# A new slot order, a tail written out by hand, and part of the x1 and weight splitting on GpSimd, in a fused attention and mixture-of-experts kernel

## The reference

```python
# x [8, 256, 128] f32, w_qkv [384, 128], w_out [128, 128], 16 heads of 8, window 128
q, k, v = split(x @ w_qkv.T)                       # to heads
att = where(sliding_window_mask, q @ k.T / sqrt(8), -inf)
x1 = layernorm(x + (softmax(att) @ v) @ w_out.T)
# mixture of 8 experts over the 2048 tokens, the best 2 by softmax(x1 @ router_w)
y = sum over e in top2: p_e * (gelu(x1 @ w_in[e] + b_in[e]) @ w_out[e] + b_out[e])
out = layernorm(x1 + y)
```

## Time and profile before

| | |
|---|---|
| median of the runs | 197.1 us |
| profiled execution, its own time | 196.5 us |
| its span, first to last instruction | 194.8 us |
| busy: PE, weight loads, DVE | 169.4, 121.5, 154.8 us |
| busy: ACT, POOL | 114.6, 84.1 us |
| mean granted TensorE clock | 0.994 of full speed |
| DMA | 17.25 MB, 35% of 16 engines' span |

### The profile page before, as it was taken

How to read it: one execution, slowest core, us unless ns; L and a number is a source line. 1 busy time by engine, 2 the same in 40 slices (tenths; PEclk the granted TensorE clock), 3 DMA queues, 4 the chain that set the end, 5 groups by cost and what they waited for, 6 DMA issues and landing times. The chain is left out here.

```text
span 194.8 us, 6184 instructions
## 1 busy us (share of the span) xinstructions
PE 169.4 (87%) x2450; PEld 121.5 (62%) x2460; DVE 154.8 (79%) x468; ACT 114.6 (59%) x216; POOL 84.1 (43%) x157
## 2 busy tenths in 40 slices
PE   7579887988989989889999899989999979999950
PEld 3354454655656656556656544558988869999950
DVE  6985959669598698697988999635798869898793
ACT  4542056687686766876857757564353784564720
POOL 7960006556563655746738366561043002603003
PEclk9999999999999999999999999999999999999997
DMA  5589594194780882955901000000000000020011
GB/s 142 148 232 222 168 242 132 53 212 125 158 226 11 176 206 72 214 160 110 218 13 57 2 8 0 3 0 0 5 0 0 3 27 27 0 59 0 3 53 54
DMA packets 23127, 17.25 MB, mean 89 GB/s; under 512 B 1827, under 2 KB 21179, under 8 KB 23099
## 3 DMA queue, kind: packets, MB, share of 16 engines
q1 hardware_dynamic: 23099, 16.87, 35.2%
HBM read 9.35 MB, written 7.34 MB: 86 GB/s over the span
## 5 line engine op out<-in xcount | busy, mean ns | idle before, releaser
L486 ACT ACTIVATE probs<-st 128x768 f32<-128x768 f32 x59 | 47.9, 811 | 23.8 <-PE st L1067 20.6
L443 POOL TENSOR_SCALAR_AFFINE_SELECT probs<-probs 128x1024 f32<-128x1024 f32 x32 | 35.1, 1097 | 57.4 <-ACT probs L486 57.3
L713 DVE TENSOR_REDUCE max_parts<-score_banks 128x2 f32<-128x384 f32 x64 | 32.6, 550 | 4.6 <-PE score_banks L1041 4.2
L594 ACT ACTIVATE hid<-score_banks,b_in_sb 128x512 f32<-128x512 f32 x32 | 21.9, 687 | 21.0 <-PE score_banks L1173 20.9
L716 DVE TENSOR_REDUCE max_parts<-score_banks 128x4 f32<-128x512 f32 x32 | 20.6, 686 | 13.6 <-PE score_banks L1041 13.6
L1067 PE MATMUL st<-stack 51*64 51x256 bf16 (+1 forms) x472 | 21.2, 254 | 6.2 <-ACT probs L486 5.7
L1030 PE MATMUL score_banks<-edges,ident_bf 64*64 64x256 bf16 (+1 forms) x192 | 19.0, 296 | 4.5 <-DVE max_parts L713 3.4
L1089 PE MATMUL o_bank<-probs,v 128*32 128x256 f32 x256 | 20.4, 391 | 0.0
L445 POOL TENSOR_SCALAR_AFFINE_SELECT probs<-probs 128x512 f32<-128x512 f32 x32 | 20.3, 634 | 0.0
L1067 PEld LDWEIGHTS st<-stack 51*64 51x64 bf16 (+1 forms) x472 | 8.6, 104 | 18.7 <-ACT probs L486 11.8
L860 DVE SCALAR_TENSOR_TENSOR x_rows<-st,gate,x_rows 128x128 f32<-128x128 f32 x64 | 18.1, 344 | 2.4 <-PE st L1187 2.0
(11 more groups left out here) (136 smaller groups left out, 331.2 us busy)
## 6 DMA issues: line engine op xcount, KB each, us to landing
stack<-scratch SPq DMA_DIRECT2D x28, 192.0 KB, 4.0
scratch<-parts SPq DMA_DIRECT2D x16, 192.0 KB, 4.0
scratch<-parts SPq DMA_DIRECT2D x24, 128.0 KB, 3.8
x_rows<-x SPq DMA_DIRECT2D x4, 256.0 KB, 5.6
out<-y_sb SPq DMA_DIRECT2D x8, 128.0 KB, 1.8
x_t_sb<-x_t SPq DMA_DIRECT2D x3, 256.0 KB, 4.8
w_in_sb<-w_in SPq DMA_DIRECT2D x1, 512.0 KB, 5.8
w_out_sb<-w_out SPq DMA_DIRECT2D x1, 512.0 KB, 7.9
```

The lines of the kernel that those rows point to most:

```text
L443: pool.affine_select(out=own, in_=own, compare_op=ALU.is_ge, fill=0.0, base=0, pattern=[[0, 2], [0, 4], [1, P]], channel_multiplier=-1).th ...
L486: nc.scalar.activation(probs[g][:, :, two, :].rearrange("p k j c -> p j k c"), pair_banks(PAIRS * b + p)[:, :, 0:3 * P].rearrange("p j (k ...
L594: nc.scalar.activation(hid[e % 2][:, :], hid_bank[e % 2], ACT.Gelu_apprx_tanh, bias=b_in_sb[:, e:e + 1]).then_inc(gelu_done, 1)
L713: nc.vector.tensor_reduce(top[:, 1, r, pair:pair + 2], bank[:, 0:384].rearrange("p (h c) -> p h c", h=2), X_AXIS, ALU.max, negate=True).th ...
```

## The change

The slot constants move, and the loops of PE, ACT, DVE and POOL end at slot 63. What came in slots 64 to 74 is written out in an order of its own on each engine, and `keep_warm` in it is gone. In the loop, PE does a slot's `scores` ahead of its `turned_scores`, and DVE a slot's maxima ahead of everything else. The turned output moves to misc[0], the turned attention, x1 and logits to misc[1] (of the last batch, x1 to misc[0]), with the waits that go with it. POOL takes `split_x1` of batches 0 to 4 (`share_x1`, in slot 6, two slots behind `turn_x1` in slot 4), and the weight splitting in eight pieces, one expert each, in slots 46 to 60; the load of `w_in` gets a semaphore of its own. DVE keeps `split_x1` of batches 5, 6 and 7.

```diff
-TURN_MAX, VALUES, S2, PV = 8, 12, 11, 15
-COPY_O, TURN_O, TURN_ATTN, PROJECT_OUT, TURN_X1, LOGITS = 22, 23, 25, 26, 30, 31
-PROJECT_QK, STACK = -14, -8
+TURN_MAX, VALUES, S2, PV = 8, 10, 11, 15
+COPY_O, TURN_O, TURN_ATTN, PROJECT_OUT, TURN_X1, LOGITS, SHARE_X1 = 21, 22, 23, 24, 28, 30, 30
+PROJECT_QK, SUBTRACT, STACK = -14, -12, -8
+WEIGHT_SLOTS = (46, 48, 50, 52, 54, 56, 58, 60)
...
# POOL
+            def share_x1(b):
+
+                cols = slice(b * T, (b + 1) * T)
+                pool.wait_ge(x1_copied, b + 1)
+                pool.tensor_copy(x1_hi[:, cols], x1_t[:, :]).then_inc(x1_hi_done, 1)
+                pool.wait_ge(x1_hi_done, b + 1)
+                pool.tensor_tensor(x1_lo[:, cols], x1_t[:, :], x1_hi[:, cols].bitcast(F32), ALU.subtract).then_inc(x1_lo_done, 1)
+
+            def split_weights(e):
+
+                pool.wait_ge(w_in_loaded, 16)
+                pool.tensor_copy(w_in_hi[:, e, :], w_in_sb[:, e, :]).then_inc(w_hi_done, 1)
+                pool.wait_ge(w_hi_done, e + 1)
+                pool.tensor_tensor(w_in_lo[:, e, :], w_in_sb[:, e, :], w_in_hi[:, e, :].bitcast(F32), ALU.subtract).then_inc(w_lo_done, 1)
...
-            for slot in range(LAST_S2 + 2):
+            for slot in range(LAST_S1 + 1):
...
-                b = batch_at(slot, PROJECT_OUT + 1)
+                b = batch_at(slot, PROJECT_OUT + 2)
                 if b is not None:
                     first_deviation(b)
-
+                b = batch_at(slot, SHARE_X1)
+                if b is not None:
+                    share_x1(b)
+                if slot in WEIGHT_SLOTS:
+                    split_weights(WEIGHT_SLOTS.index(slot))
+
+            late, last = B - 2, B - 1
+            for g in range(2, QUADS):
+                mask_probs(late, g)
+            first_deviation(late - 1)
+            for g in range(QUADS):
+                mask_probs(last, g)
+            first_deviation(late)
...
# ACT
-                for offset, piece in ((TURN_MAX, copy_max), (TURN_ATTN, copy_attention), (PROJECT_QK, take_top), (PROJECT_QK + 1, take_middle),
-                                      (VALUES, pad_v), (COPY_O, copy_output), (TURN_X1, copy_x1), (LOGITS, copy_logits)):
+                for offset, piece in ((TURN_MAX, copy_max), (PROJECT_QK, take_top), (VALUES + 1, pad_v), (SUBTRACT, take_middle),
+                                      (TURN_X1 + 1, copy_x1), (COPY_O, copy_output), (LOGITS, copy_logits), (TURN_ATTN, copy_attention)):
...
+            copy_max(last)
+            exponentials(late, 5)
+            exponentials(late, 6)
+            exponentials(late, 7)
+            pad_v(last)
+            route_exponentials(EARLY, 1)
+            act.wait_ge(moe_w_loaded, 16 * 2)
+            exponentials(last, 0)
+            exponentials(last, 1)
+            copy_output(late)
+            exponentials(last, 2)
+            exponentials(last, 3)
+            exponentials(last, 4)
+            exponentials(last, 5)
+            copy_attention(late)
+            exponentials(last, 6)
+            exponentials(last, 7)
...
# DVE, the loop now
+            for slot in range(LAST_S1 + 1):
...
# take_maxima, take_low (SUBTRACT + 1), normalise (TURN_O), split_max (TURN_MAX - 1),
# first_residual (PROJECT_OUT), first_stats and first_moments (+ 1), first_norm (TURN_X1 - 1)
...
+            route_shift(EARLY, B // 2 - 1)
+            first_residual(late - 1)
+            first_stats(late - 1)
+            first_moments(late - 1)
+            choose(EARLY, 1, 0)
+            choose(EARLY, 1, 1)
+            first_norm(late - 1)
+            normalise(late)
+            choose(EARLY, 1, 2)
+            choose(EARLY, 1, 3)
+            first_residual(late)
+            first_stats(late)
+            first_moments(late)
+            first_norm(late)
+            split_x1(late - 1)
             add_expert(0, 0)
-            split_x1(B - 2)
             add_expert(0, 1)
-            normalise(B - 1)
+            split_x1(late)
+            normalise(last)
...
# PE, waits of the moved pieces
 turn_max:        -logits_copied b - 2 (b >= 3)      +normed 4 * b - 4 (b >= 2)
 turn_output:     -v_padded 4 * b + 8                +part_low b + 5 (b < 4), max_copied b + 2 (b < 7)
 turn_attention:  -max_copied b + 3                  +v_padded 4 * b + 8 (b = 0, 6), logits_copied b
 turn_x1:         -part_low b + 6                    +v_padded 4 * b + 12 (b < 5), resid_done, logits_copied
 first_layer(c, 0):                                  +x1_lo_done 2 * c + 2
...
# PE, the tail now
+            turn_max(last)
+            turned_scores(late, 5)
+            project_out(late - 1)
+            turned_scores(late, 6)
+            turned_scores(late, 7)
+            weigh_values(late, 1)
+            project_v(last)
+            weigh_values(late, 2)
+            turned_scores(last, 0)
+            turned_scores(last, 1)
+            weigh_values(late, 3)
+            turned_scores(last, 2)
+            turned_scores(last, 3)
+            pe.wait_ge(w_lo_done, NX)
+            first_layer(0, 0)
+            turn_output(late)
+            turned_scores(last, 4)
+            weigh_values(last, 0)
+            turned_scores(last, 5)
+            turn_attention(late)
+            turned_scores(last, 6)
+            turned_scores(last, 7)
+            weigh_values(last, 1)
+            project_out(late)
+            weigh_values(last, 2)
             first_layer(0, 1)
+            turn_x1(late - 1)
+            pe.wait_ge(moe_w_loaded, 16 * 2)
             second_layer(0, 0)
-            weigh_values(B - 1, QUADS - 1)
+            route_logits(late - 1)
+            weigh_values(last, 3)
             unit(0, 2)
```

More of the change, by code:

```diff
@@ L584, in _ @@
                         piece(b)
-                if slot == LAST_S1 + 3:
-                    route_exponentials(EARLY, 1)
+            late, last = B - 2, B - 1
+            copy_max(last)
[15 more added lines that the diff above has]
+            exponentials(last, 7)
             def gelu(c, e):
@@ L612, in _ @@
             gelu(0, 0)
+            copy_x1(late - 1)
             gelu(0, 1)
-            copy_output(B - 1)
+            copy_logits(late - 1)
+            copy_output(last)
             gelu(0, 2)
-            copy_x1(B - 2)
+            copy_x1(late)
             gelu(0, 3)
-            copy_logits(B - 2)
+            copy_logits(late)
             gelu(0, 4)
-            copy_attention(B - 1)
+            copy_attention(last)
             gelu(0, 5)
@@ L821, in _ @@
                 take_odd(n)
-            for slot in range(LAST_S2 + 1):
-                b = batch_at(slot, TURN_O + 1)
+            for slot in range(LAST_S1 + 1):
+                n = jobs_at(slot)
+                if n is not None:
+                    take_maxima(*n)
+                b = batch_at(slot, SUBTRACT + 1)
+                if b is not None:
+                    take_low(b)
+                b = batch_at(slot, TURN_O)
                 if b is not None:
                     normalise(b)
+                b = batch_at(slot, TURN_MAX - 1)
+                if b is not None:
+                    split_max(b)
+                b = batch_at(slot, PROJECT_OUT)
+                if b is not None:
+                    first_residual(b)
                 b = batch_at(slot, PROJECT_OUT + 1)
@@ L1107, in turn_max @@
                 turned = misc[0][:, :].bitcast(BF16)
[L1108 to L1111 removed]
+                if b >= 2:
+                    pe.wait_ge(normed, 4 * b - 4)
+                else:
+                    pe.wait_ge(part_low, b + 3)
                 pe.wait_ge(max_split, b + 1)
@@ L1226, in _ @@
             pe.wait_ge(consts_ready, 7)
-            for slot in range(LAST_S2 + 1):
+            for slot in range(LAST_S1 + 1):
+                n = jobs_at(slot)
+                if n is not None:
+                    scores(*n)
                 n = pair_at(slot)
@@ L1233, in _ @@
                     keep_warm(2)
-                n = jobs_at(slot)
-                if n is not None:
-                    scores(*n)
                 b = batch_at(slot, TURN_MAX)
@@ L1262, in _ @@
                     project_v(b)
+                b = batch_at(slot, SUBTRACT)
+                if b is not None:
+                    subtract_top(b)
                 b = batch_at(slot, TURN_X1)
@@ L1265, in _ @@
                     turn_x1(b)
-                b = batch_at(slot, TURN_O)
-                if b is not None:
-                    turn_output(b)
                 b = batch_at(slot, LOGITS)
@@ L1273, in _ @@
                     route_logits(b)
+                b = batch_at(slot, TURN_O)
+                if b is not None:
+                    turn_output(b)
                 n = quad_at(slot)
```

115 lines of the change are left out of this document (41 added, 74 removed).

## The result

The changed kernel takes 189.16 us (median of 4, 188.12 to 189.32) beside 197.08 (196.51 to 197.11): a ratio of 0.960, with a 95% interval of 0.957 to 0.962. I had forecast 191.3 in a range of 187.5 to 195.0. Direction and range held; the gain is 7.9 us where I had 5.8. The profiled execution took 189.22 us (span 187.5), so its parts are compared with those of the profiled 196.5 (span 194.8).

A forecast was written before the change was run, and what follows sets the result against it. PE was taken as the nearest bound in the loop and the bound in the experts, the tail as a chain of short waits. Terms -1.65, +0.1, +0.2, -3.9 sum to -5.25: 196.5 to 191.25, forecast 191.3, range 187.5 to 195.0.

The forecast's parts named there:

- Part 1: Loop order: 3.4 us of PE waits for maxima go, ACT's overfull slot 5 adds 1.75; -1.65 us, ends -7 and +2.
- Part 2: Loop, batches 0 to 4: moving split_x1 from DVE to POOL is worth 0 by itself.
- the loop closes up too: Rival, chance 0.14: PE's idle time in the loop also shrinks, 3 us more gain, giving 188.3.
- Part 3: POOL's x1 copy and subtract in the loop: 1.2 us for both, hidden behind other work, cost 0.
- Part 4: POOL's eight weight pieces, slots 46 to 60: 0.73 us each, cost 0 to +1, taken as +0.1 us.
- Part 5: DVE and POOL contention, mainly at split_max: up to 0.46 us each, +0.2 us in all, ends 0 and +3.
- Part 6: Hand-ordered tail: 15.0 us from turned maxima to first second-layer matmul, against 19.73; -3.9 us, ends -5 and -1.
- Part 7: Experts, other semaphores and the start (slots 0 to 10, project_v(0) ahead of the first turned scores): each 0.
- the first rival: Rival, chance 0.20: only the tail gains and the loop's waits merely move, giving 193.2 with the 0.6 added.
- The tail only: Rival, chance 0.20: the loop's waits move instead of going, since ACT's slot 5 is overfull; 193.2 us.
- it doesn't do what it says: Rival, chance 0.05: x1 moves nothing, the tail keeps its 19.7 us, the loop gains 0.3; 196.3 to 196.8.
- Slower: Rival, chance 0.10: POOL paces the loop, share and weights in slots 6 and 7 delaying a mask; +9, 200 us.

The follow-up runs named there:

- the three together: Changed kernel with filler ahead of scores (slots 1 to 10) and in slots 11 to 14, weights loaded at slot 25, batch 4's x1 on DVE: 186.93 us.
- the kernel with the first filler: Changed kernel with the two filler matmuls of slots 1 to 10 put ahead of the slot's scores instead of behind: 188.73 us.
- the kernel with both fillers: Changed kernel with filler ahead of the scores in slots 1 to 10 and two more filler matmuls in each of slots 11 to 14: 187.74 us.

## Why the prediction was right and wrong

- **Part 1, the order (-1.65; measured with all of the loop -3.11).** The waits of 3.4 us for L713 went, as said; 0.9 for L768 came, 0.3 of it in the loop. The term of +1.75 us was the mis-sized one: it added ACT's durations, where queued instructions start up to 0.1 us before the one ahead has ended (0.71 for one of 0.81). I had ACT free 2.20 us after the slot's L1067; it was free at 1.98 (78.95 to 80.93), which leaves 0.11 of the 0.35 us a batch, 1.2 us over five batches. I had no term for PE's order, which halves its waits for the exponentials (0.7 us). With x1 (0.6) and the 1.0 us of slot 63 against them, this makes up most of the 2.1 us by which the loop beat its forecast; the rest isn't divided. I had also treated DVE's order as a part with a price of its own. It has none: with the old offsets it costs 8 us (6 to 7 without the clock's share), and the new offsets with the old order make the loop 3.4 us longer than before (87.8 against 84.4). Of the combinations that were run only the pair gains.
- **Part 2, x1 off DVE (0).** Right for the old loop (0.9993), but my argument was made on the old loop. In the new one DVE's time is worth some 0.6 us, by one execution at a high clock on each side. That agrees with "the loop closes up too", of which a piece came true.
- **Part 3, POOL's prices (1.2 us for the two).** Measured: 0.40 and 0.73, so 1.13. That the mask behind the share is "hidden" held for PE's values, but not at slot 63, where the masks run into `split_max`.
- **Part 4, the weights (+0.1).** Measured 0.29 + 0.46 a piece, as said. Two of PE's waits for masks (0.41 and 0.32 us, at 85.8 and 91.7) follow such pieces. Moving the pieces away gains 0.4 between medians, within the noise and within the end of +1.
- **Part 5, contention (+0.2, ends 0 and +3).** The mechanism was right, the size was not: one place costs about a microsecond, once the weights and the share have made POOL late, since the DVE pair stands directly ahead of a PE wait with nothing to cover it. A rule of the Trainium skill (SBUF — State Buffer, section on two separate sides) describes the pair of ports as a lock held for a whole instruction; 0.91 and 0.55 us, each ending with POOL's mask, agree with it.
- **Part 6, the tail (-3.9).** 13.8 us instead of 15.0 from the turned maxima on. The term mis-sized is that of the exponentials, 0.87 each, for the reason of part 1: they take 8.3 us and not 9.6. The mechanism, a chain of waits in the slots' order that a hand-written order shortens, agrees with ACT's waits (6.7 to 1.1 us). But PE, whose work I had at 13.6, now comes nearest to being full.
- **Part 7, the start (0).** "`project_v(0)` comes ahead of the first turned scores instead of after: 0" left out that the filler also moved, from ahead of a slot's scores to behind them. Behind a waiting matmul it fills nothing. PE's busy time at 14 to 16 us fell from 1.98 to 1.33. In three of four executions of the change the mean clock is 0.979 to 0.982, and in the profiled one it fell to 1.2 GHz at 16 us, about 1.1 of the 1.65 us. This was the real miss: the diff showed it, and I read only what computes.
- **The sum.** It gives 191.25 for the scale of the profiled execution. The median stands 0.6 above that, which I wrote and did not add (the first rival's 193.2 has it): 191.9 would have been consistent. That the total came within 2.1 us is partly luck, since the start's 1.65 hides as much of what loop and tail gained; without it the result would lie at the lower end of the range.
- **The clock in the tail** stayed at 1.00, as said.
- **The rivals.** The measured 189.16 is nearer to "the loop closes up too" (188.3) than to my 191.3, but its mechanism came true in part only: PE's idle time in the loop fell from 9.8 to 7.5 us. "The tail only" is out, as the loop gained 3.11. So is "it doesn't do what it says". "Slower" was looked for at the right engine, but POOL did not pace the loop: it was without a pause only at 83 to 107 us, and that cost a few tenths there and the 1.0 us at its end.
- **The signs.** No wait for L713, POOL over 90 us and the clock in the tail came as written. The full batches took 12.2 and 11.9 us, not 12.7, and the tail 13.8, not 15. One sign of being wrong came as well, small: PE waiting for POOL's masks, 1.1 us.

Open: how the tail's 6.1 us divide among the orders of PE, ACT and DVE, the banks that changed places and the weight splitting that left DVE there (1.13 + 1.22 us), since only the filler was tested by itself; where the 0.7 us lie by which the three together miss their forecast; an "issue" gap of 0.6 us ahead of L1196, near 97.5 us, that the changed kernel and others show and that nothing in the trace explains; and why the clock's fall comes in some executions of a kernel and not in others.

## What to carry to other kernels

Price a queue on an engine by the distance between starts in the trace, not by durations. Change the order within a slot and the offsets between slots as one thing: either half alone can cost as much as the pair gains (the new order with old offsets 8 us, the new offsets with the old order nearly the whole 7.9). Filler only fills if it stands ahead of the instruction that waits, and when the order of a loop is changed, ask of each filler what it stands behind now. Keep other work, GpSimd's as well as VectorE's own, away from the spot where VectorE's last small instructions release the bound engine.

## What the runs showed of the hardware

Two things were new to me. One is how far the clock's fall travels. PE had been busy 2.15, 2.42 and 2.73 of 4 us around where it fell in the change, in the kernel with the first filler and in that with both; it then stood at 0.50 in a stretch of 2 us and was back at 1.00 within about 4; in the change that costs about 1.1 us. In these three traces, with one hole more filled in each, the fall came at 16 us, then 34, then 108. It is no fixed answer to a hole: two traces with the same 2.15 of 4 us at the start kept 1.00, and of the kernel with both fillers three executions of four have a mean of 0.991 or more. The other is that an ACT instruction can start 0.1 us before the trace ends the one ahead of it, which made the tail's eleven exponentials 1.3 us shorter than I had counted. Beside these, a VectorE instruction of 0.19 us with two inputs took 0.91 and 0.55 us next to GpSimd's masks, and released TensorE 1.0 us late.
